# Moving V's store and class loads to the end of a batch, and a second buffer for the rows that are scattered to the experts

## The chip, the cores and the metric

The kernel runs on one core of one Trainium2 chip. The time is device time in microseconds (us) of one execution, and lower is better. A core has four compute engines, each with its own instruction queue that it works through in order: PE (TensorE, matrix products into PSUM), DVE (VectorE), ACT (ScalarE) and POOL (GpSimd). SP (SyncE) computes nothing here. It issues nearly all DMAs, and when it waits for a semaphore, every DMA behind that wait in its queue waits too. POOL issues the indirect DMAs, those whose destination rows are given by a list.

## The reference, cut to what matters

A block of attention with a gate, a layer norm, then a mixture of eight experts and a second layer norm. There are 16 batches of 512 tokens with 256 features and 16 heads of 16. Each token attends to 39 fixed distances back: 0 to 32 ("near") and 48, 64, 96, 128, 192, 256 and 384 ("far").

```python
scores = jnp.stack([jnp.einsum('bhnd,bhnd->bhn', q, _shift(k, delta, n)) for delta in OFFSETS], axis=-1) * scale
scores = scores + pos_bias.T[None, :, None, :]
alpha = jax.nn.softmax(scores, axis=-1)
for i, delta in enumerate(OFFSETS):
    out = out + alpha[..., i:i + 1] * _shift(v, delta, n)
gate = jax.nn.sigmoid(x @ Wgate + bgate)
return flat * gate @ Wout + bout
...
logits = jax.nn.relu(x @ rw1 + rb1) @ rw2 + rb2
vals, ids = jax.lax.top_k(logits, K)                 # K = 2
disp = jnp.zeros((E, CAP, Cx), x.dtype).at[ids_f, pos_c].add(xr * keep[:, None])
h = jax.nn.relu(jnp.einsum('enc,ech->enh', disp, ew1) + eb1[:, None, :])
eo = jnp.einsum('enh,ehc->enc', h, ew2) + eb2[:, None, :]
y = eo[ids_f, pos_c] * (probs_f * keep)[:, None]
...
x = _layernorm(x + _L0_attn_ref(x, L0_attn_Wqkv, ...), axis=-1)
x = _layernorm(x + _L0_ffn_ref(x, L0_ffn_rw1, ...), axis=-1)
```

## The kernel before

**Stages.** `attention` handles the 16 batches one after another, as a software pipeline, and leaves each token's normed row in DRAM twice: in `xln` (float32), and as a row of `disp`, at the place of its expert. `experts` then multiplies the rows of `disp` expert by expert, `combine` adds and norms. The change touches only `attention`, which is some three quarters of the time.

**The order of the work.** An iteration of the pipeline has 16 slots. `SLOTS_OF` says which steps stand in which slot, `AHEAD` to which batch a step belongs: in iteration i the projections are those of batch i+1 (`proj`), the max pass that of batch i+1 (`maxp`), scores and values those of batch i, the output product and layer norm those of batch i-1 (`outp`), the router that of batch i-1 (`rout`), ranks and scatters those of batch i-2 (`rank`). `run_iterations` writes each engine's instructions in that order. PE takes a step in its own slot, the other engines one slot later (or as `LATER` says). The engines keep pace by semaphores alone. Batch numbers of even and odd kind use two sets of buffers where a tile is a list (`n.par`).

**The steps that matter here, in the order of one iteration.**
- The max pass (`maxp` near0 to near3, far0, far1). For each block PE opens two PSUM banks with a bias matmul (L679) and adds many small products of q and k (L689). DVE reduces both banks (L954, L958). There are three banks (`gp`) for all such work, taken in turn. So near2 takes the last free bank and the one that DVE gives back when it has reduced the first half of near1.
- The far values. PE multiplies the far weights with `v_far` (L623) in slots 2 and 4. ACT copies them out of PSUM to `o_far`. They lie in another order of rows than the near ones, so SP stores them to `o_dram` (L442, four DMAs) and loads them back in the right order to `o_back` (L445). DVE's merge (L898) adds them to the near values into `ob`; the first merge of a batch waits for `o_back`.
- V. The projection leaves V in the tile `vs`. SP loads it to `v_near` (L434, 16 DMAs, at slot 1), stores it to `v_dram` (L459), waits until that has landed, and loads `v_far` from it in rows by class (L466, four DMAs). Before, these last two steps stand in SP's queue right behind the loads of q and k (`qs`, `ks`, L486) and ahead of `o_dram`.
- The mask rows. The maxima go through `m_dram` to one row of `qs` (L492, L496) at slot 12.
- The layer norm's end. ACT writes the normed rows to `y32` (L854, four instructions), then their float16 high part to `y16` (L859), and DVE the low part (L979). L859 may overwrite `y16` only when the scatters of the batch before have read it, and so waits for them.
- The scatters. POOL issues eight indirect DMAs a batch from `y16` to `disp` (L1095), behind the four small instructions of the layer norm of the next batch, and right before ACT's L859 of that batch is due.
- The gate. DVE computes the divisor and its reciprocal in the tile `oden` (L932, L937, each in two halves), and `og = ob * 1/oden` (L922).

These are the two waits of L859 and DVE's instruction behind it:

```python
wait(act, scattered, n.at(128))
...
act.wait_ge(y_ready, n.at(4, 4))
nc.scalar.copy(y16[:, :, 0:D], y32[:, :, :]).then_inc(yh_ready, 1)
...
dve.wait_ge(yh_ready, n.at(1, 1))
nc.vector.tensor_tensor(y16[:, :, D:2 * D], y32[:, :, :], y16[:, :, 0:D], ALU.subtract).then_inc(yl_ready, 1)
```

## Time and profile before

| | us |
|---|---|
| median of three runs | 2224.62 |
| the three runs | 2222.07 to 2226.25 |
| the profiled execution | 2221.11 |
| its span in the profile | 2219.4 |
| PE busy | 1547.7 (70%) |
| DVE busy | 968.8 (44%) |
| ACT busy | 907.2 (41%) |
| POOL busy | 662.7 (30%) |
| mean granted PE clock, share of 2.4 GHz | 0.774 |

The profile lists every instruction with its start and length. Where an engine stood idle, it also names what ended the wait, as in `[4.61 <-DVE m_near L954]`: 4.61 us idle until DVE's instruction of line 954 was done. "issue" as a cause means that the profile shows nothing that the engine waited for. In SP's rows the length is that of issuing the DMA, not of moving the data. L numbers are lines of the kernel before; after the change they are smaller by one from L310 on, and by other amounts further down (L859 is then L858, L679 is L678).

### The profile page before, as it was taken

Reading aid. Unit: us, or ns where it says so; the run is one execution under the profiler, and the core shown is the slowest. Engines: PE = TensorE matmul, PEld = TensorE weight load, DVE = VectorE, ACT = ScalarE, POOL = GpSimd, SP = SyncE. Lnnn points to the kernel's source line nnn. Section 1 sums busy time; section 2 is a strip of 40 time slices with the busy share of each in tenths; the row PEclk is TensorE's granted clock in tenths of the full one; section 3 lists DMA queues with packets and bytes.
Section 4 is the critical chain, followed back from the end, with each engine's and each line's share of the span. In section 5 each row is a group of like instructions: output and inputs, shape, how many; then the busy total and the mean of one; then the engine's idle time right before and its main releaser. Section 6 shows DMA issues by size and latency. Waiting matters only on the chain. (4 is left out here: it accounts for less than half of the span.)

```text
span 2219.4 us, 76239 instructions
## 1 busy us (share of the span) xinstructions
PE 1547.7 (70%) x33280; PEld 1043.3 (47%) x33280; DVE 968.8 (44%) x1925; ACT 907.2 (41%) x1544; POOL 662.7 (30%) x654
## 2 busy tenths in 40 slices
PE   0456686867768686867679686867864499999900
PEld 0234454545445454545445454545542267676700
DVE  4214354444534453544545354544533355555422
ACT  1132262534434262534435252534432365656323
POOL 4121232324141333324142333324132122323232
PEclk9676686868777796868778686868776699999955
DMA  2473433525151533425151523416010434444255
GB/s 79 95 207 98 99 77 84 97 71 122 47 123 37 114 66 85 88 70 104 49 125 42 101 66 78 96 47 128 22 44 12 126 75 108 86 104 89 28 136 184
DMA packets 238550, 194.80 MB, mean 88 GB/s; under 512 B 66847, under 2 KB 231727, under 8 KB 238080
## 3 DMA queue, kind: packets, MB, share of 16 engines
q1 hardware_dynamic: 222896, 175.11, 32.8%
q0 software_dynamic: 15360, 15.10, 4.2%
q8 instruction: 266, 4.36, 0.8%
q14 instruction: 28, 0.23, 0.0%
HBM read 98.07 MB, written 86.18 MB: 83 GB/s over the span
## 5 line engine op out<-in xcount | busy, mean ns | idle before, releaser
L395 POOL TENSOR_TENSOR p<-p 128x512 f16<-128x512 f32 x96 | 135.0, 1406 | 604.1 <-ACT p L791 563.0
L805 ACT COPY featT<-gp 128x1024 f16<-128x1024 f16 x96 | 93.4, 1032 | 354.2 <-PE gp L540 354.2
L395 DVE TENSOR_TENSOR p<-p 128x512 f16<-128x512 f32 x96 | 95.0, 990 | 286.5 <-ACT p L791 286.2
L547 PE MATMUL gp<-featT,wr 128*128 128x512 f16 x768 | 192.9, 409 | 24.1 <-DVE mT L947 18.2
L623 PE MATMUL o<-v_near,p 128*32 128x34 f16 (+1 forms) x6144 | 161.6, 185 | 36.3 <-issue 33.6
L623 PEld LDWEIGHTS o<-v_near,p 128*32 128x32 f16 x6144 | 153.7, 98 | 54.4 <-issue 51.2
L1387 PE MATMUL up<-rowsT,w 128*128 128x512 f16 x768 | 172.9, 386 | 8.8 <-DVE w L1464 5.3
L1401 PE MATMUL dn<-w,h 128*128 128x256 f16 x1536 | 170.1, 273 | 0.0
L1349 POOL DMA_INDIRECT xln<-y,place x64 | 104.9, 1640 | 217.5 <-DVE y L1491 176.7
L790 ACT ACTIVATE p<-st 128x512 f16<-128x512 f32 x192 | 116.6, 607 | 107.6 <-PE st L591 103.4
L1401 PEld LDWEIGHTS dn<-w,h 128*128 128x128 f16 x1536 | 149.7, 98 | 17.3
L1095 POOL DMA_INDIRECT disp<-y,sidx x128 | 126.7, 990 | 76.7 <-issue 49.4
L898 DVE TENSOR_TENSOR ob<-o,o_back 128x272 f32<-128x272 f32 x64 | 28.1, 439 | 260.9 <-DMA o_back<-o_dram 159.8
L1448 ACT ACTIVATE h<-up,b 128x512 f16<-128x512 f32 x128 | 88.1, 689 | 129.9 <-PE up L1387 73.1
L547 PEld LDWEIGHTS gp<-featT,wr 128*128 128x128 f16 x768 | 76.0, 104 | 123.8 <-issue 33.4
L1387 PEld LDWEIGHTS up<-rowsT,w 128*128 128x128 f16 x768 | 75.9, 99 | 99.9 <-issue 11.3
L591 PE MATMUL st<-qs,ks 49*64 49x32 f16 (+1 forms) x4096 | 104.3, 195 | 23.2 <-issue 23.2
L1503 DVE TENSOR_TENSOR h<-h 128x512 f16<-128x512 f32 x128 | 88.7, 693 | 69.6 <-ACT h L1449 69.6
L1082 POOL TENSOR_TENSOR x<-xin,x 128x1024 f16<-128x1024 f32 x16 | 34.0, 2128 | 281.2 <-ACT x L812 281.2
L791 ACT ACTIVATE p<-st 128x512 f32<-128x512 f32 x192 | 118.0, 615 | 0.0
L679 PE MATMUL gp<-near_bias,sel 32*128 32x512 f16 x96 | 28.9, 561 | 125.8 <-DVE m_near L954 124.3
L547 PE MATMUL gp<-wout,featT 128*128 128x256 f16 x384 | 79.2, 400 | 50.7 <-ACT featT L805 50.7
(173 smaller groups left out, 3067.1 us busy)
## 6 DMA issues: line engine op xcount, KB each, us to landing
qk_dram<-qk SPq DMA_DIRECT2D x64, 256.0 KB, 2.5
v_near<-vs SPq DMA_DIRECT2D x224, 66.0 KB
qs<-qk_dram SPq DMA_DIRECT2D x96, 128.0 KB, 4.6
ks<-qk_dram SPq DMA_DIRECT2D x96, 128.0 KB, 7.6
o_dram<-o_far SPq DMA_DIRECT2D x64, 136.0 KB
o_back<-o_dram SPq DMA_DIRECT2D x16, 544.0 KB
v_dram<-vs SPq DMA_DIRECT2D x16, 528.0 KB, 9.5
v_far<-v_dram SPq DMA_DIRECT2D x64, 132.0 KB
```

What stands on the lines that cost most here:

```text
L395: engine.tensor_tensor(p16[:, b, 1, :], p32[:, b, :], p16[:, b, 0, :], ALU.subtract).then_inc(is_split, 1)
L547: last = nc.tensor.matmul(dst, lhs(a, c), rhs(b, c), start=(k == 0), stop=(k == len(todo) - 1))
L591: last = nc.tensor.matmul(banks[e][64 * u + first:64 * (u + 1), P * z + BLOCK * b:P * z + BLOCK * (b + 1)], key[rows[e], p, lo - BLOCK + f ...
L623: last = nc.tensor.matmul(dst[quad, :, 2 * z + e, 0:cols.stop - cols.start], p16[:, 2 * (k % 2) + e, a, c:c + BLOCK], v[:, :, 2 * z + e, c ...
L790: nc.scalar.activation(p16[:, b, 0, :], bank[:, :], ACT.Exp)
L791: nc.scalar.activation(p32[:, b, :], bank[:, :], ACT.Exp).then_inc(exp_ready, 1)
L805: gp_done(nc.scalar.copy(featT[:, i, :, :].rearrange("f c t -> f (c t)"), bank[:, :].bitcast(F16)), n, stage, PART_OF_T[stage], i)
L1095: nc.gpsimd.indirect_dma_start(out=disp[:, :], out_offset=bass.IndirectOffsetOnAxis(ap=sidx[:, t, k:k + 1], axis=0), in_=y16[:, t, :].bitc ...
L1349: nc.gpsimd.indirect_dma_start(out=xln[:, :], out_offset=bass.IndirectOffsetOnAxis(ap=place[:, gr, t:t + 1], axis=0), in_=y[:, gr, t, :], ...
L1387: last = nc.tensor.matmul(up[h % 4][:, :], w1[e.par][:, a, c, P * h:P * (h + 1)], rowsT[:, gr, b, c, :], start=(k == 0), stop=(k == 5))
L1401: last = nc.tensor.matmul(dn[u][:, D * (t % 2):D * (t % 2 + 1)], h16[:, gr, a, h, P * t:P * (t + 1)], w2[e.par][:, b, h, :], start=(k == 0 ...
L1503: nc.vector.tensor_tensor(h16[:, gr, 1, h, :], h32[:, h % 2, :], h16[:, gr, 0, h, :], ALU.subtract).then_inc(h_lo, 1)
```

## The change

There are three parts.

1. V's store and class loads (`v_dram`, `v_far`) leave the step `proj vg1` and become `move_v`, called at the end of SP's step `maxp t`, behind the mask rows. They serve the same batch as before, and in the same iteration, eight slots later.
2. `y16` becomes a list of two tiles, taken in turn by the batch's number. ACT's L859 now waits for the scatters of the batch before the last (`n.at(128, -128)` in place of `n.at(128)`).
3. The tile `oden` goes. The gate's divisor and reciprocal are computed in `og` itself; in return the first divisor, no longer the product, waits for `og_lo` (that POOL has read the old `og`). It gives back the room that the second `y16` takes.

```diff
-        y16 = sb("y16", [P, TILES, ROW], F16)
+        y16 = [sb(f"y16_{i}", [P, TILES, ROW], F16) for i in range(2)]
-        oden = sb("oden", [P, TILES * H, HD], FP32)
...
             def proj(n, part):
-                if part == "vg0":
+                if part[:2] != "qk":
                     return
-                if part == "vg1":
-                    wait(sp, v_far_in, n.at(64, -64))
-                    sp.wait_ge(v_split, n.at(TILES, TILES))
-                    sync.dma_start(v_dram[n.par]...).then_inc(v_stored, 16)
-                    sp.wait_ge(v_stored, n.at(16, 16))
-                    wait(sp, pv_done, n.at(UNIT_PAIRS, FAR_PAIRS - UNIT_PAIRS))
-                    for u in range(2):
-                        for v in range(2):
...
             def maxp(n, part):
...
+                move_v(n)
+
+            def move_v(n):
+                wait(sp, v_far_in, n.at(64, -64))
+                sp.wait_ge(v_split, n.at(TILES, TILES))
+                sync.dma_start(v_dram[n.par]...).then_inc(v_stored, 16)
+                sp.wait_ge(v_stored, n.at(16, 16))
+                wait(sp, pv_done, n.at(UNIT_PAIRS, FAR_PAIRS - UNIT_PAIRS))
+                for u in range(2):
+                    for v in range(2):
...
-                    wait(act, scattered, n.at(128))
+                    wait(act, scattered, n.at(128, -128))
-                    nc.scalar.copy(y16[:, :, 0:D], y32[:, :, :]).then_inc(yh_ready, 1)
+                    nc.scalar.copy(y16[n.par][:, :, 0:D], y32[:, :, :]).then_inc(yh_ready, 1)
...
                 if part == "mul":
-                    wait(dve, og_lo, n.at(1))
...
                     if first == 0:
                         dve.wait_ge(eg_ready, n.at(TILES, TILES))
-                        wait(dve, og_ready, n.at(1))
+                        wait(dve, og_lo, n.at(1))
```

The other uses of `y16` (PE's transposes, DVE's low part and the tail with token and weights, POOL's scatters) take `y16[n.par]`; the clearing of `disp` takes `y16[0]`.

SP's queue, inside the loop, from the loads of q and k of the next batch to the mask rows. Before, V's two steps stand ahead of `o_dram`:

```order
L486 DMA qs<-qk_dram 16x8x512 x6
L486 DMA ks<-qk_dram 16x8x512 x6
L459 DMA v_dram<-vs 128x4x528
...
L466 DMA v_far<-v_dram 32x16x132 x4
...
L442 DMA o_dram<-o_far 128x1x272 x4
...
L445 DMA o_back<-o_dram 128x4x272
...
L501 DMA xln<-y 128x4x256
...
L450 DMA xres<-in_L_attn_x 128x4x256
...
L492 DMA m_dram<-mT 16x512
L496 DMA qs<-m_dram 1x4096 x2
```

After, at the same place of SP's queue:

```order
L471 DMA qs<-qk_dram 16x8x512 x6
L471 DMA ks<-qk_dram 16x8x512 x6
...
L441 DMA o_dram<-o_far 128x1x272 x4
...
L444 DMA o_back<-o_dram 128x4x272
...
L500 DMA xln<-y 128x4x256
...
L449 DMA xres<-in_L_attn_x 128x4x256
...
L477 DMA m_dram<-mT 16x512
...
L481 DMA qs<-m_dram 1x4096 x2
L488 DMA v_dram<-vs 128x4x528
...
L495 DMA v_far<-v_dram 32x16x132 x4
```

V's two steps moved past the way of the far values, the rows of the layer norm, the residual's load and the mask rows, and now stand ahead of the load of x and of `v_near` of the next iteration.

ACT, in an iteration written out ahead of the loop (an even batch), from the copy of the transposed rows to the next exponentials. Before:

```order
L805 COPY featT<-gp1 128x1024
L854 ACTIVATE y32<-y32,nmr,rstd 128x256 x4
L859 CAST y16<-y32 128x4x256
L790 ACTIVATE p16<-st0 128x512
L791 ACTIVATE p32<-st0 128x512
```

After:

```order
L804 COPY featT<-gp1 128x1024
L853 ACTIVATE y32<-y32,nmr,rstd 128x256 x4
L858 CAST y16_0<-y32 128x4x256
L789 ACTIVATE p16<-st0 128x512
L790 ACTIVATE p32<-st0 128x512
```

Nothing moved there; only the buffer of the copy is one of two, and an odd batch takes `y16_1`.

## Rows read from the trace of the kernel before

**Rows 1.** Waits of PE, 232:1630 us: total us, times, longest:
```profile
PE gp L679 <- DVE m_near L954: 105.5, 28, 13.5
PE gp L689 <- issue: 54.9, 83, 2.0
```

**Rows 2.** Waits of ACT, 232:1630:
```profile
ACT y L859 <- DMA disp<-y,sidx: 152.6, 13, 14.2
```

**Rows 3.** Timeline of PE, one batch: start, us, instruction, [idle before <- who ended it]:
```profile
856.34 0.76 PE L689 MATMUL gp<-ks,qs 16*32 16x64 f16 x58 [1.17 <-issue]
861.71 0.61 PE L679 MATMUL gp<-near_bias,sel 32*128 32x512 f16 x2 [4.61 <-DVE m_near L954]
...
864.39 0.61 PE L679 MATMUL gp<-near_bias,sel 32*128 32x512 f16 x2 [1.40 <-DVE m_near L954]
```

**Rows 4.** Timeline of DVE, the same batch:
```profile
855.22 0.44 DVE L898 TENSOR_TENSOR ob<-o,o_back 128x272 f32<-128x272 f32 x1 [12.38 <-DMA o_back<-o_dram]
859.83 1.23 DVE L979 TENSOR_TENSOR y<-y 128x1024 f16<-128x1024 f32 x1 [4.17 <-ACT y L859]
860.97 1.28 DVE L954 TENSOR_REDUCE m_near<-gp 128x8 f16<-128x512 f32 x2
```

**Rows 5.** Timeline of ACT, the same batch:
```profile
844.02 2.07 ACT L854 ACTIVATE y<-y,nmr,rstd 128x256 f32<-128x256 f32 x4 [10.15 <-POOL nmr L1078]
858.75 1.04 ACT L859 CAST y<-y 128x1024 f16<-128x1024 f32 x1 [12.66 <-DMA disp<-y,sidx]
```

**Rows 6.** Timeline of POOL, first and last of eight scatters:
```profile
844.83 1.11 POOL L1095 DMA_INDIRECT disp<-y,sidx  x1 [0.84 <-issue]
...
853.89 0.97 POOL L1095 DMA_INDIRECT disp<-y,sidx  x1 [0.30 <-issue]
```

**Rows 7.** Timeline of SP's queue, the same batch:
```profile
831.99 0.38 SPq L459 DMA_DIRECT2D v_dram<-vs  x1
...
844.44 2.77 SPq L442 DMA_DIRECT2D o_dram<-o_far  x4
850.71 0.39 SPq L445 DMA_DIRECT2D o_back<-o_dram  x1
...
890.25 0.54 SPq L496 DMA_DIRECT2D qs<-m_dram  x2
...
903.17 12.51 SPq L434 DMA_DIRECT2D v_near<-vs  x16
920.21 5.65 SPq L474 DMA_DIRECT2D qk_dram<-qk  x4
```

**Rows 8.** The line that stores v_dram (L459):
```profile
DMA to landing us min/median/max: 8.7/9.5/12.7
```

**Rows 9.** Timeline of PE, the first two batches:
```profile
170.72 0.61 PE L679 MATMUL gp<-near_bias,sel 32*128 32x512 f16 x2 [15.20 <-DVE m_near L954]
...
257.76 0.61 PE L679 MATMUL gp<-near_bias,sel 32*128 32x512 f16 x2 [7.97 <-DVE m_near L954]
...
259.92 0.61 PE L679 MATMUL gp<-near_bias,sel 32*128 32x512 f16 x2 [0.88 <-DVE m_near L954]
```

**Rows 10.** Timeline of PE, product for q and k:
```profile
908.71 0.29 PE L564 MATMUL st<-sel,far_bias 64*128 64x256 f16 x2 [2.85 <-ACT p L791]
...
912.13 7.71 PE L547 MATMUL gp<-featT,wqk 128*128 128x512 f16 x24
```

**Rows 11.** Timeline of POOL, near the end:
```profile
1641.10 1.15 POOL L395 TENSOR_TENSOR p<-p 128x512 f16<-128x512 f32 x1 [4.28 <-ACT p L791]
```

**Rows 12.** Timeline of ACT, the last batch:
```profile
1708.27 1.04 ACT L859 CAST y<-y 128x1024 f16<-128x1024 f32 x1 [12.52 <-DMA disp<-y,sidx]
```

**Rows 13.** Timeline of SP's queue, the next two o_back:
```profile
954.80 0.39 SPq L445 DMA_DIRECT2D o_back<-o_dram  x1
...
1051.83 0.39 SPq L445 DMA_DIRECT2D o_back<-o_dram  x1
```

**Rows 14.** Windows of 5 us (busy us of each engine, granted PE clock, DMA):
```profile
910.00:915.00 5.00, 3.81 (x71) 1.74 (x72) 3.15 (x1) 0.00 (x0) 0.79 (x1) 0.51 0.36 82
```

More of the change, by code:

```diff
@@ L496, in maxp @@
                     sync.dma_start(qs[n.par][r:r + 1, :, :], m_dram[n.par][PAIRS * e:PAIRS * (e + 1), :].unsqueeze(0)).then_inc(m_in[n.par], 16)
+                move_v(n)
+            def move_v(n):
+                wait(sp, v_far_in, n.at(64, -64))
+                sp.wait_ge(v_split, n.at(TILES, TILES))
+                sync.dma_start(v_dram[n.par].rearrange("(t p) c -> p t c", p=P), vs[n.par][:, :, :, :].rearrange("p t h c -> p t (h c)")).then_inc(v_stored, 16)
+                sp.wait_ge(v_stored, n.at(16, 16))
+                wait(sp, pv_done, n.at(UNIT_PAIRS, FAR_PAIRS - UNIT_PAIRS))
+                for u in range(2):
+                    for v in range(2):
+                        r, h = 64 * u + BLOCK * v, 8 * u + 4 * v
+                        src = v_dram[n.par][:, h * VW:(h + 4) * VW].rearrange("(a r) c -> a r c", r=FAR_STEP)
+                        sync.dma_start(v_far[r:r + BLOCK, :, u, v, :, :].rearrange("a r h c -> a r (h c)"), src).then_inc(v_far_in, 16)
             def outp(n, part):
@@ L928, in gate @@
                         dve.wait_ge(eg_ready, n.at(TILES, TILES))
-                        wait(dve, og_ready, n.at(1))
+                        wait(dve, og_lo, n.at(1))
                     dve.wait_ge(merged, n.at(TILES, end))
                     weight = ob[:, :, :, HD:OW].rearrange("q t h c -> q (t h) c")[:, heads, :]
-                    nc.vector.scalar_tensor_tensor(oden[:, heads, :], eg[n.par][:, heads, :], 1.0, weight.to_broadcast([P, H * (end - first), HD]),
+                    nc.vector.scalar_tensor_tensor(og[:, heads, :], eg[n.par][:, heads, :], 1.0, weight.to_broadcast([P, H * (end - first), HD]),
                                                    ALU.add, ALU.mult).then_inc(og_step, 1)
@@ L1118, in sem @@
             return ctx.enter_context(nc.semaphore(name))
-        ident, zero_rows = g["ident"], a["y16"]
+        ident, zero_rows = g["ident"], a["y16"][0]
         near_vec, far_vec = g["near_vec"], g["far_vec"]
```

25 lines of the change are left out of this document (10 added, 15 removed).

## The prediction

> **What bounds the kernel now.** Start with the page. No engine is near full: PE is busy for 70% of the span, DVE and ACT for less. So waits set the time of the attention stage, and they have to be read batch by batch. A batch takes about 100 us there, and the stage lasts roughly from 60 to 1720 us. The chain of waits on the page is no help: it ends in the last stage and reaches back only to 2129 us. I therefore went to the waits of PE, the engine that does most and whose order is fixed. In the 14 batches from 232 to 1630 us PE's largest wait is that of L679, the bias matmul that opens a block of the max pass, for DVE's reduction L954: 105.5 us in 28 waits. The second is not for anything the profile names: 54.9 us of "issue" before the small matmuls of L689 [rows 1]. ACT's wait at L859 for the rows that are scattered is 152.6 us in 13 batches, 11.7 us each [rows 2].
>
> Now follow one batch back from L679. PE finishes the block near1 at 857.1 us (856.34 + 0.76) and starts near2 only at 861.71, after 4.61 us [rows 3]. It waits for DVE's reduction of near1, which begins at 860.97. In front of that reduction, in DVE's order, stand two other instructions: L898, which waited 12.38 us for o_back, and L979, which waited 4.17 us for ACT's L859 [rows 4]. L859 stood 12.66 us until the scatters of the batch before had landed [rows 5]; POOL had begun to issue them at 844.83 and ended at 854.86 [rows 6]. So two waits lie one behind the other in front of DVE's reduction: o_back until 855.22, then the scatters until 858.75. The later one decides, and that is the scatters. From L859 to near2 it is always the same 3.0 us (861.71 - 858.75).
>
> **The two buffers.** With them L859 waits for the scatters of two batches ago, which ended about 90 us earlier. It then follows the four L854 at 846.1 us (844.02 + 2.07) and ends at 847.1. That cover is long; this wait is gone in every batch from the third on.
>
> **V's moves.** They decide when o_back comes. Now SP issues v_dram at 831.99, holds until it has landed, issues the four v_far, only then the four o_dram (844.44) and at 850.71 o_back, which lands 4.5 us later [rows 7]. Without V's steps SP can issue o_dram right at 832, as o_far was copied by then. It queues behind the ks loads exactly as v_dram does now, which lands after 9.5 us [rows 8], at 841.5. I take the same for o_dram: o_back issued at about 842 and landed at about 846.5, that is 8.7 us earlier. DVE then does the merge at 846.9, L979 by 848.4, and is idle before near1 is finished.
>
> So near2 waits for near1 itself and the first half of its reduction. An idle DVE makes that wait 0.88 us (at 259.92) [rows 9].
>
> **Where V's steps go.** They now stand behind the mask rows (890.25) [rows 7]. Issued at about 891, with at most the longest landing of any v_dram, 12.7 us [rows 8], and 2.9 us for v_far (from 841.5 to 844.44 now), SP is free at 906.6, or at 903.4 with the median. What stands behind them in SP's queue: the load of x, needed most of a batch later, and v_near, which starts at 903.17 now since it waits for PE. v_near takes 12.5 us of issue and ends 4.5 us before qk_dram is issued (920.21). So up to 4.5 us of delay are covered, and the longest landing makes 3.4 plus 0.4 for the load of x. The class products that need v_far come after the product that ends at 919.8 [rows 10]; v_far is issued by 906.6 and has 13 us to land. I put the move at nothing in the new place.
>
> **The gate in place** has the same four instructions and the same sizes. The wait for og_lo moves one step forward to work that ended tens of us before. Nothing.
>
> **What a batch gains.** The 28 waits of [rows 1] are 14 pairs. One pair is that of 257.76 and 259.92 (7.97 and 0.88) [rows 9]; in the other 13 the second wait is 1.40 [rows 3], together 18.2. That leaves 78.5 us for 13 first waits, 6.0 each. If each becomes 0.88 and each second one too, a batch gains 5.2 + 0.5 = 5.7 us. This is the upper end. The lower end comes from the "issue" waits. In the batch shown they end about 2 us after the last scatter was issued (854.86, and near1 ends at 857.1), and all along the scatters PE gets only a few matmuls at a time. In batches where near1 comes through early, near2 would meet the same trouble, and part of the gain is paid back. The batch shown, where near1 ends after the scatters, is not open to that: it gains 4.61 - 0.88 = 3.7 us, with the second wait 4.2. I take 3.7 for the lower end and 4.7, the middle, for the forecast: 13 x 4.7 = 61 us (48 to 74).
>
> **The batches at either end.** In the first, L679 waits 15.20 us at 170.72 for a reduction behind o_back [rows 9]. V's move brings o_back forward by 8.7 us, as in any batch. I take 9 (5 to 12). In the second there are no scatters yet, and 7.97 becomes 0.88: 7 us. In the last batch that has scores, POOL waited 4.28 us for ACT's exponentials behind L859 [rows 11]; its scatters had ended by 1636.8: 4 us. In the last of all nothing else runs: L859 waited 12.52 us [rows 12], and the router, the last scatters and the start of the experts all follow it. 12.5 us in full.
>
> **Sum:** 61 + 9 + 7 + 4 + 12.5 = 93.5 us. The profiled execution took 2221.1 us (span 2219.4), the sum makes it 2127.6. The median of the runs is 2224.6, 3.5 above it, so my forecast is **2131 us**, 4.2% less.
>
> **Rivals.**
>
> *The clock takes it back, or doubles it.* Batches differ although their work is the same: from o_back to o_back one takes 104.1 us and the next 97.0 [rows 7, 13]. One reason in view is the product for q and k. In the long batch it ran from 912.13 for 7.71 us, while from 910 to 915 the granted clock was 0.51, the lower of the two levels (1.2 GHz); PE had waited 2.85 us for ACT just before [rows 10, 14]. The change shifts every phase, so all batches could be long ones (about 3.5 us more than the mean, 13 x 3.5 = 46: 2177) or short ones (2085). The waits in front of that product are not touched, which speaks for no change. 0.12 and 0.10.
>
> *POOL's scatters are slowed by DVE.* Now DVE is idle while POOL issues them, from 842.8 to 855.2. After the change the merge (0.44), L979 (1.23), the reduction (1.28) and a split fall into these 10 us. If each held POOL for its whole length, the last scatter would come 3 to 4 us later, and the "issue" waits with it: 13 x 3.5 = 45 us of the gain lost, 2176. No row shows a DVE instruction beside a scatter in this stage, so it can't be excluded, and the length that I give it, 3.5 us, is that of these instructions. 0.10.
>
> The Trainium skill has the rule that speaks for this case (SBUF — State Buffer, section "SBUF: two separate sides"): DVE and GpSimd share a pair of ports under an exclusive lock, and descriptors written by GpSimd starve while DVE holds it. The section names DVE operations with two SBUF inputs only against a GpSimd operation that reads SBUF; by that, of the four, only L979 and the split could count, and the time would be about 2156, an estimate from their lengths; no row here shows it.
>
> *The wait for o_back stays.* If o_dram lands late (it is four DMAs where v_dram is one), the merge could come at 852 instead of 847. DVE would still be done with L979 and ready at about 853.7, before near1 ends at 857.1. It costs only the batches where near1 comes early, about 2 us in five of them: 2141. Inside the range. So V's move by itself should be worth only the two first batches, some 16 us, and the buffers the rest; this is a point the experiments can test.
>
> *Slower than before.* V's steps in the new place hold SP, and v_near, the q/k store, the key loads and PE's near0 shift in turn. Each us beyond the cover of 4.5 costs one us a batch. To eat the 93.5 us it needs 7.2 us in each of 13 batches on top of the cover: SP free no earlier than 914.9, 24 us after v_dram was issued, where the longest landing and the issue in the trace make 15.6. At 10 us beyond the cover the time would be 2261. 0.04.
>
> **How the numbers follow.** Forecast with its own spread of 2110 to 2155: 0.62. Scatters slowed 0.10, all batches long 0.12, all short 0.10, slower 0.04, and 0.02 for no change by a cause I don't see. The range of eight in ten goes from 2092 to 2178. About 0.2% is what a measurement of this kernel can tell from no change. Faster by more: 0.93; within: 0.02; slower: 0.05.
>
> **What would show it.** In the profile of the changed kernel ACT's L858 must have no wait for the scatters; o_back must land about 2 us after the values of near0, not 11; the wait of L678 for the reduction must be near 0.9 us in place of 6.0, with "issue" waits as before; and the batch must take about 95 us. If "issue" waits in front of the small matmuls grow by as much as the waits for DVE shrink, the scatters are the bound and my lower end is too high. If the scatters take longer than 10.0 us for eight, DVE slows them. If PE waits more for ks, V's steps hold SP. It would be wrong altogether if PE had another chain of the same length behind DVE's reduction, which I do not find in its waits.

## The result, and the profile after

| | us |
|---|---|
| kernel before, median of the runs beside it | 2223.35 |
| kernel after, median of four runs | 2152.39 (2149.35 to 2154.96) |
| ratio after to before, 95% interval | 0.9681 [0.9661, 0.9702] |
| span of the profiled execution, before and after | 2219.4 and 2152.9 |

The change saves 71 us, 3.2%. The forecast was 2131, so the sign is right and the time is within the range, but it is 21 us above the forecast: of the 93.5 us expected 22 did not come (27 by the two spans).

First the waits of PE from 232 to 1630 us in the kernel after, the same view as [rows 1] (total us, times, longest). L678 is the bias matmul, L688 the small matmuls, L952 DVE's reduction:

```profile
PE gp L678 <- DVE m_near L952: 66.2, 28, 7.2
PE gp L688 <- issue: 54.1, 93, 1.2
```

The wait for DVE fell from 105.5 to 66.2 us, the "issue" waits stayed where they were (54.9). The wait of ACT for the scatters [rows 2] is gone from the list. Two rows are new. "remote" is what the view says when a semaphore's increment ended the wait, but the instruction that makes this increment had ended long before:

```profile
DVE m_near L952 <- remote: 60.2, 9, 8.5
ACT p L789 <- remote: 11.1, 9, 2.2
```

Now one batch of the kernel after, at the place of [rows 3 to 6]. ACT (L853 is the normed rows, L858 the float16 copy):

```profile
817.33 2.07 ACT L853 ACTIVATE y<-y,nmr,rstd 128x256 f32<-128x256 f32 x4 [10.09 <-POOL nmr L1076]
819.43 1.04 ACT L858 CAST y<-y 128x1024 f16<-128x1024 f32 x1
```

POOL, the first, third and last of the eight scatters:

```profile
818.14 1.10 POOL L1093 DMA_INDIRECT disp<-y,sidx  x1 [0.85 <-issue]
...
820.83 1.75 POOL L1093 DMA_INDIRECT disp<-y,sidx  x1 [0.30 <-issue]
...
827.99 0.97 POOL L1093 DMA_INDIRECT disp<-y,sidx  x1 [0.30 <-issue]
```

DVE (L897 merge, L977 low part, L952 reduction of near1):

```profile
819.61 0.44 DVE L897 TENSOR_TENSOR ob<-o,o_back 128x272 f32<-128x272 f32 x1 [3.45 <-DMA o_back<-o_dram]
820.51 1.23 DVE L977 TENSOR_TENSOR y<-y,y 128x1024 f16<-128x1024 f32 x1 [0.46 <-issue]
830.35 1.29 DVE L952 TENSOR_REDUCE m_near<-gp 128x8 f16<-128x512 f32 x2 [8.61 <-PE gp L688]
```

PE, the end of near1, and near2:

```profile
821.72 0.44 PE L688 MATMUL gp<-ks,qs 16*32 16x64 f16 x26 [0.24 <-issue]
...
828.59 0.27 PE L688 MATMUL gp<-ks,qs 16*32 16x64 f16 x5 [1.16 <-issue]
830.04 0.24 PE L688 MATMUL gp<-ks,qs 16*32 16x64 f16 x2 [1.19 <-issue]
831.10 0.61 PE L678 MATMUL gp<-near_bias,sel 32*128 32x512 f16 x2 [0.81 <-DVE m_near L952]
```

Both waits of the old chain are gone: L858 follows L853 without a wait, the merge comes 1.5 us after the first scatter instead of 10.4 (855.22 - 844.83), and DVE is done by 821.7. Then it waits 8.61 us for PE. PE issues its matmuls two to eight at a time with gaps of 0.45 to 1.19 us, until 1.1 us after the last scatter was issued (828.96). near2 opens 13.0 us after the first scatter.

The batch before it shows the other face of the same thing. There near1 comes through (PE), and DVE begins late:

```profile
728.35 0.27 PE L688 MATMUL gp<-ks,qs 16*32 16x64 f16 x4 [0.48 <-issue]
734.99 0.60 PE L678 MATMUL gp<-near_bias,sel 32*128 32x512 f16 x2 [6.37 <-DVE m_near L952]
```

```profile
724.68 1.23 DVE L977 TENSOR_TENSOR y<-y,y 128x1024 f16<-128x1024 f32 x1 [3.58 <-issue]
734.24 1.29 DVE L952 TENSOR_REDUCE m_near<-gp 128x8 f16<-128x512 f32 x2 [8.34 <-remote]
```

The eight scatters of this batch stand from 722.32 to 733.13. near1 is finished at 728.6 (the view models the ends of matmuls) and DVE is idle, yet its reduction begins at 734.24, 1.1 us after the last scatter again. DVE could not begin earlier: the trace records the semaphore increment that it waits for at 734.22, 5.6 us after the end of the matmul that makes it. Outside the scatters such an increment stands at most 0.09 us after its matmul's end in this trace; in the nine batches with a "remote" wait of DVE it comes 2.2 to 6.4 us late. I call this time, from some 1.5 us after the first scatter until 1.1 us after the last, **the window**. In 10 of 13 batches near2 opens 12.7 to 13.1 us after the first scatter. In the other three it slips in before, and then near3 waits until 13.0 to 13.4 us. Before the change near2 opened 16.0 us after it on the mean.

Where the 66.5 us of the two spans lie, by the start of scatters in POOL's timeline:

| stretch | before | after | saved | forecast |
|---|---|---|---|---|
| start to the first scatter (343.32, 336.12) | 343.3 | 336.1 | 7.2 | 16 |
| 12 batches, to 1543.90 and 1496.72 | 1200.6 | 1160.6 | 40.0 | 56 |
| the 13th and the last with scores (to 1694.27, 1640.24) | 150.4 | 143.5 | 6.9 | 8.7 |
| the last of all (to its last scatter) | 48.9 | 37.7 | 11.3 | 12.5 |
| the later stages | 476.2 | 475.0 | 1.2 | 0 |

### The profile page after: what moved, and what is told of

The parts are those of the page before. It is cut to its first block and busy times, and to the rows that moved or that the text cites. A ratio compares the mean times of both kernels' runs of the same rounds, so it can differ in the third digit from the quotient of the medians.

```text
span 2152.9 us, 76230 instructions
## 1 busy us (share of the span) xinstructions
PE 1557.9 (72%) x33280; PEld 1048.6 (49%) x33280; DVE 961.3 (45%) x1925; ACT 907.2 (42%) x1544; POOL 673.1 (31%) x654
## 3 DMA queue, kind: packets, MB, share of 16 engines
q8 instruction: 266, 4.36, 0.9%
## 5 line engine op out<-in xcount | busy, mean ns | idle before, releaser
L804 ACT COPY featT<-gp 128x1024 f16<-128x1024 f16 x96 | 93.5, 1034 | 439.0 <-PE gp L539 439.0
L394 DVE TENSOR_TENSOR p<-p 128x512 f16<-128x512 f32 x96 | 85.4, 890 | 297.3 <-ACT p L790 297.1
L546 PE MATMUL gp<-featT,wr 128*128 128x512 f16 x768 | 195.5, 413 | 24.5 <-DVE mT L945 18.2
L789 ACT ACTIVATE p<-st 128x512 f16<-128x512 f32 x192 | 116.8, 608 | 120.8 <-PE st L590 105.5
L1093 POOL DMA_INDIRECT disp<-y,sidx x128 | 137.6, 1075 | 65.3 <-issue 48.9
L952 DVE TENSOR_REDUCE m_near<-gp 128x8 f16<-128x512 f32 x128 | 81.9, 682 | 156.6 <-PE gp L688 96.3
L874 ACT ACTIVATE hid<-gp,br 128x512 f16<-128x512 f32 x128 | 88.8, 694 | 63.5 <-PE gp L546 60.4
L546 PE MATMUL gp<-featT,wqk 128*128 128x512 f16 x384 | 111.9, 461 | 1.4 <-ACT featT L804 1.2
```

The costliest lines, as they stand in the source:

```text
L394: engine.tensor_tensor(p16[:, b, 1, :], p32[:, b, :], p16[:, b, 0, :], ALU.subtract).then_inc(is_split, 1)
L546: last = nc.tensor.matmul(dst, lhs(a, c), rhs(b, c), start=(k == 0), stop=(k == len(todo) - 1))
L789: nc.scalar.activation(p16[:, b, 0, :], bank[:, :], ACT.Exp)
L804: gp_done(nc.scalar.copy(featT[:, i, :, :].rearrange("f c t -> f (c t)"), bank[:, :].bitcast(F16)), n, stage, PART_OF_T[stage], i)
L874: nc.scalar.activation(hid16[:, 0, ht, :], bank[:, :], ACT.Relu, bias=br1[:, ht:ht + 1], scale=1.0 / WS)
L1093: nc.gpsimd.indirect_dma_start(out=disp[:, :], out_offset=bass.IndirectOffsetOnAxis(ap=sidx[:, t, k:k + 1], axis=0), in_=y16[n.par][:, t, ...
```

## Experiments: the two halves of the change

**Buffers alone.** V's two steps put back where they stood:

```diff
                 if part == "vg1":
+                    wait(sp, v_far_in, n.at(64, -64))
+                    sync.dma_start(v_dram[n.par]...).then_inc(v_stored, 16)
...
-                move_v(n)
```

> The changed kernel with V's two steps put back ahead of o_dram; two y16 buffers and the gate in place stay. Theory A (the step of the prediction): the wait of ACT for the scatters was the later of two, so the buffers alone carry all batches with scatters, and V's move is worth the first two batches, about 16 us: 2168 us, 2160 to 2176. In the trace DVE's merge waits for o_back until 8 to 10 us after the first scatter, as before, and near2 opens 12.7 to 13 us after it, as in the changed kernel. Theory B: o_back decides as soon as the scatter wait is gone, then near2 opens later than 13 us and the time is above 2185 us.

Measured: 2151.43 us against 2228.18, ratio 0.965 [0.9628, 0.9671]. The time is that of the whole change, and 9 us below the range of the expectation, which had given about 16 us to V. From first scatter to first scatter a batch takes 95.3 us here and 96.7 in the kernel after: 17 us less in the 12 batches, against 12 us more at the start (first scatter at 348.2 here, at 336.1 after). One batch, DVE and PE (L895 merge, L950 reduction, L676 bias, L686 small matmuls):

```profile
833.60 0.44 DVE L895 TENSOR_TENSOR ob<-o,o_back 128x272 f32<-128x272 f32 x1 [12.50 <-DMA o_back<-o_dram]
```

```profile
826.15 0.60 PE L686 MATMUL gp<-ks,qs 16*32 16x64 f16 x11 [0.32 <-issue]
836.07 0.60 PE L676 MATMUL gp<-near_bias,sel 32*128 32x512 f16 x2 [9.32 <-DVE m_near L950]
```

PE finishes near1 at 826.75 and then waits 9.32 us for DVE, whose merge waits for o_back. In the kernel after o_back comes in time, and PE loses the same time to the window. In this batch one wait stands where the other stood. In seven of the 13 batches near2 opens earlier here, 8.9 to 10.9 us after the first scatter, and in the other six at 13.0 to 15.4.

The window itself is not in this trace, though the same rows are scattered at the same place. Among scatters that stand from 632.23 to 642.27, near1 comes in one piece:

```profile
635.18 0.78 PE L686 MATMUL gp<-ks,qs 16*32 16x64 f16 x64
```

The "issue" waits in front of the small matmuls are 8.9 us here, from 232 to 1630, and 54.1 in the kernel after; there is no "remote" wait of DVE. The next section comes back to this.

**V's move alone.** One `y16`, with the old wait:

```diff
-            y16 = [sb(f"y16_{i}", [P, TILES, ROW], F16) for i in range(2)]
+            y16 = [sb("y16", [P, TILES, ROW], F16)] * 2
-                    wait(act, scattered, n.at(128, -128))
+                    wait(act, scattered, n.at(128))
```

> The changed kernel with one y16 buffer and the old wait for the scatters of the batch before; V's move and the gate in place stay. Theory A: only the first two batches gain, about 16 us: 2207 us, 2200 to 2214, and L859's wait (here L858) stays near 11 us a batch, near2 opens about 16 us after the first scatter. Theory B (o_back decides): most of the 71 us are here, below 2180 us.

Measured: 2214.39 us against 2228.18, ratio 0.9951 [0.9927, 0.9975]: 14 us saved by the medians and 11 by the ratio, where the prediction had 16. ACT:

```profile
849.06 1.04 ACT L858 CAST y<-y 128x1024 f16<-128x1024 f32 x1 [10.66 <-DMA disp<-y,sidx]
```

PE:

```profile
838.12 0.61 PE L678 MATMUL gp<-near_bias,sel 32*128 32x512 f16 x2
852.02 0.61 PE L678 MATMUL gp<-near_bias,sel 32*128 32x512 f16 x2 [12.49 <-DVE m_near L952]
```

Again 3.0 us from L858 to near2, as in the kernel before. This confirms the chain of the prediction: with one buffer the scatters decide, however early o_back is. near2 opens 14.9 us after the first scatter (837.14). The parts do not add: 78 for the buffers and 11 for V by these ratios, 71 for both. (The kernel after was measured in another group of runs than these two; more on that below.)

**The gate in place alone.** The kernel before with `oden` gone and nothing else.

> The kernel before with the gate computed in place alone (one buffer, V's steps in their old place). Every theory: no change, 2222 to 2228 us, ratio 1.000 within 0.002, since the four instructions keep their sizes and the wait for og_lo falls on work that ended tens of us before. A difference of over 0.3% would mean that the in-place operands cost DVE or that the wait is not free.

Measured: 2227.24 us against 2226.28, ratio 1.000 [0.9978, 1.0023]. It costs nothing, as put down. But its trace has no window either: the "issue" waits in front of the small matmuls are 5.0 us from 232 to 1630, where the kernel before has 54.9. At one buffer this makes no difference to the time, as PE then waits for the scatters through L859 in any case.

## Experiments: what the window is

**No scatters.** The loop's scatters are left out but for those of the last batch; the waits for them go too. So the experts read rows that were not written.

```diff
+                    if not (n.i is None and n.c == B - 1):
+                        return
-                    wait(act, scattered, n.at(128, -128))
-                    wait(dve, scattered, n.at(128))
```

> The changed kernel, without the eight scatters of every batch but the last (the waits for them go too), and with one more wait between the two groups of adds in the expert stage; so only the attention stage up to the last batch is to be read. Theory C: while POOL's eight scatters run, PE and DVE get their next instructions late, and this window of 10.8 us is the floor that kept near2 at 12.7 us after the first scatter. Then without scatters near2 opens within 4 us of the place where the first scatter stood, the issue waits in front of the small matmuls of L688 fall from 54 us in 14 batches below 15, DVE's waits labelled remote vanish, and a batch takes 87 to 90 us in place of 96.7. Theory D: the late instructions come from the other DMAs around it (o_back, xln, xres) and not from the scatters: the issue waits stay above 40 us and a batch takes 95 us or more.

Measured in one run: 2052.28 us. From o_back to o_back a batch takes 89 us, there is no "remote" wait, and the longest wait for L952 is 3.3 us. So the kernel without scatters takes 100 us less than the kernel after, 7 us or so a batch, though no engine waits for one there. The experts' later stages are no part of this: from the last scatter to the end it is 474 to 478 us in this run, in the three below and in the kernel after.

**Small rows.** The same 128 indirect DMAs, with 64 bytes of each row to a table of its own in place of the 1040 to `disp`. What the experts read is again left out.

```diff
-                            out=disp[:, :], ...
-                            in_=y16[n.par][:, t, :].bitcast(U32), ...
+                            out=g["thin"][:, :], ...
+                            in_=y16[n.par][:, t, 0:32].bitcast(U32), ...
```

> The changed kernel with the same eight scatters a batch, the same number of rows and indices, but 64 bytes of each row in place of 1040, written to a table of their own; the rows of the experts stay empty, and the expert stage has one more wait between its adds, so only the attention stage is to be read. If the bytes in the DMA queues delay the instructions (theory C1), it looks like the kernel without scatters: batch 87 to 91 us, issue waits of L688 below 20 us. If the making of the descriptors on POOL or their number does it (theory C2), it looks like the changed kernel: batch 95 to 98 us, issue waits of L688 near 54 us, near2 at 12 us or later after the first scatter.

Measured in one run: 2060.80 us. POOL does the same work (eight scatters in 10.8 to 11.4 us, the third again 1.8 us), but near2 opens 4.3 us after the first. PE in the middle of the eight (782.41 to 793.75):

```profile
786.69 0.61 PE L679 MATMUL gp<-near_bias,sel 32*128 32x512 f16 x2 [2.37 <-DVE m_near L953]
787.22 0.74 PE L689 MATMUL gp<-ks,qs 16*32 16x64 f16 x64
788.85 0.61 PE L679 MATMUL gp<-near_bias,sel 32*128 32x512 f16 x2 [0.88 <-DVE m_near L953]
```

All 64 matmuls in one piece. So POOL's work, the number of its rows, and a lock between POOL and DVE do not make a window by themselves: all three are here, and it is not.

**Half rows and quarter rows.** The same, with 512 and with 256 bytes.

> As the kernel with 64 B of each row scattered to a table of its own, now with 512 B of each row (the experts again read rows that the loop did not scatter, and the output is not the reference's). 1040 B to disp gave 2152 us, 64 B gave 2061. Theory C1 in its proportional form (what starves PE is the volume of the scattered rows): half the volume, half the loss, about 2105 us, with starts of DVE delayed less often. Theory C1 with a threshold (the 16 DMA engines must be full for the starving; at half the bytes their queues drain between two scatters): 2060 to 2075 us and no DVE start late by over 2 us. Theory of the destination (writes into disp are what costs, not their size; both this and the 64 B one write elsewhere): 2061 us as well, so a time near 2105 rules both others out, a time near 2061 leaves two.

Measured in one run: 2145.46 us. All three forms of the expectation missed: with half the bytes nearly the whole loss is back (93 of 100 us). These rows too go to a table of their own, so writing to `disp` is not what it takes. PE, among scatters that stand from 720.79 to 731.92:

```profile
728.31 0.27 PE L689 MATMUL gp<-ks,qs 16*32 16x64 f16 x5 [0.48 <-issue]
729.04 0.27 PE L689 MATMUL gp<-ks,qs 16*32 16x64 f16 x6 [0.46 <-issue]
729.77 0.27 PE L689 MATMUL gp<-ks,qs 16*32 16x64 f16 x5 [0.46 <-issue]
...
733.70 0.61 PE L679 MATMUL gp<-near_bias,sel 32*128 32x512 f16 x2 [2.95 <-DVE m_near L953]
```

> As before with 64 and 512 B of each row, now 256 B (the experts again read rows that the loop did not scatter). 64 B: 2061 us, 512 B: 2145, 1040 B: 2152. The volume alone is out after those, since half of it takes nearly the whole loss. If the loss follows the size of one row with a step somewhere under 512 B: either 2060 to 2065 us (step above 256 B) or 2140 to 2150 us (step below). If it rises with the size and saturates, between: 2090 to 2125 us, with near2 opening 6 to 9 us after the first scatter where 64 B gave 4.3 and 512 B 12.8 in every second batch.

Measured in one run: 2070.74 us, near2 4.1 to 4.7 us after the first scatter in all 13 batches. So the four times fall in two pairs: 2061 and 2071 us with 64 and 256 bytes in a row, 2145 and 2152 with 512 and 1040.

**It is not the volume.** A row whose place lies beyond its expert's 1024 is dropped by the bounds check, and the trace's DMA packets carry 4 bytes for it in place of 1040. Later batches drop more and more rows: the packets of a batch's scatters hold 1.07 MB in the second batch of the kernel after, 0.62 in the sixth, 0.15 in the twelfth and 0.08 in the thirteenth. The window does not get shorter: near2 opens 13.0, 13.0 and 12.8 us after the first scatter in the first three of these, near3 13.4 us after it in the last. Three stretches of 11 us with the scatters (busy us and count of PE, PEld, DVE, ACT and POOL, granted PE clock, DMA share, GB/s). The second and the twelfth batch of the kernel after:

```profile
430.00:441.00 11.00, 4.05 (x90) 2.20 (x87) 1.58 (x2) 3.63 (x7) 8.85 (x9) 0.63 0.60 195
1402.00:1413.00 11.00, 3.57 (x96) 1.86 (x88) 1.67 (x2) 4.18 (x8) 8.87 (x9) 0.50 0.35 110
```

The second batch with 64 bytes in a row:

```profile
424.00:435.00 11.00, 6.88 (x366) 4.44 (x360) 6.11 (x9) 4.20 (x8) 8.85 (x9) 0.66 0.36 108
```

DMA share and GB/s are the same in the last two, while PE gets 96 matmuls in the one and 366 in the other.

The Trainium skill (DMA: Bandwidth & Descriptors, section "Specifications") says that a transfer under 512 B does not reach the line rate. That is about the transfer, and no run here measured the rate of these rows. The Trainium skill (SBUF — State Buffer, section "SBUF: two separate sides") also says that a DMA cannot be slowed by a compute operation, nor the other way round. In the window the single matmul keeps its length of some 0.2 us, but its start is late; whether the DMAs' traffic is what delays it, these runs do not show.

**A rival that these runs do not exclude.** The size of a row is not enough to make a window. The runs were taken in six groups, and the kernel before was timed beside each; groups 2 and 5 ran on the same chip, 75 minutes apart. By the "issue" waits in front of the small matmuls (232:1630) the window comes and goes with the group:

| group | kernels, with the issue waits in us | window |
|---|---|---|
| 1 | before 54.9, after 54.1 | yes |
| 2 | buffers only 8.9, V's move only 3.0, no scatters 3.0, 64 bytes 2.9 | no |
| 3 | gate only 5.0, slot 11 2.0, slot 11 with V back 4.8, spread 2.4 | no |
| 4 | spread with V back 7.6, first V 2.9 | no |
| 5 | 512 bytes 60.6 | yes |
| 6 | 256 bytes 1.7 | no |

Buffers only, V's move only and gate only scatter the full rows of 1040 bytes at the old place, and have no window. So two readings are left. Either the window needs rows of 512 bytes or more and something else that comes and goes with the kernel as it is built; or it comes and goes with the chip and the hour, and the pair of 2061 and 2071 against 2145 and 2152 says nothing of the size of a row. The kernel after was measured in group 1 alone, so nothing here decides between the two; it would take the kernel after and the one with 64 bytes side by side, several times. The time of the kernel before is no help: it is 2223 to 2229 us in every group, and that of gate only, without a window, is the same.

**What holds PE is open, but two candidates are weaker than they look.** The table of DMA queues has one of kind "instruction" (266 packets, 4.36 MB), so the engines' own instructions travel by DMA as well, and a refill behind the rows is a candidate. In the batch of the kernel after shown above a packet of that queue ran from 820.70 to 822.38 and the next began at 832.88; none was under way while PE was held, from 822.66 to 830.28, in which time it took 37 matmuls. In 12 of the 13 batches none is under way from 4.4 to 14.0 us after the first scatter. The other candidate is a late semaphore. It holds DVE, as said above; but of these 37 matmuls only one waits for a semaphore, and it is not in the first groups, which are as late. The last packet of the rows ends at 830.02, PE's first matmul after its last gap starts at 830.04.

## Experiments: the scatters elsewhere

With two buffers the scatters no longer have to be done before L858 of the next batch, so they can leave the max pass. `SLOTS_OF` is all that changes. The kernels of this section have no window, see the table above, and are compared below with a kernel after that has one.

**All in slot 11**, behind the max pass, and the same **with V's steps put back**:

```diff
-    6: [("outp", "w"), ("maxp", "near0"), ("rank", "s0"), ("rank", "s1")],
-    7: [("rank", "s2"), ("rank", "s3"), ("outp", "y"), ("maxp", "near1")],
+    6: [("outp", "w"), ("maxp", "near0")],
+    7: [("outp", "y"), ("maxp", "near1")],
-    11: [("maxp", "t"), ("rout", "h0")],
+    11: [("maxp", "t"), ("rout", "h0"), ("rank", "s0"), ("rank", "s1"), ("rank", "s2"), ("rank", "s3")],
```

> All eight scatters of a batch stand in slot 11 (behind the max pass) in place of slots 6 and 7; all else as in the kernel after. Theory P (place: their traffic costs because it falls on the max pass, where PE and DVE hand three banks to and fro; in slot 11 ACT's exponentials set the pace and there is slack): the window costs 2 us a batch or less in the new place, spacing of the batches about 90 to 92 us, 2152 - 13 x 5.5 = 2080 us, no waits of DVE's reduction for 'remote'. Theory A (amount: a window of 10 us costs PE the same 6 to 7 us wherever it lies): 2145 to 2155 us, with 'issue' waits on other lines of PE. A third outcome, slower than 2160, is POOL: it would be late with the splits of slot 12 and the values would wait for it (L622 for POOL).

> Scatters in slot 11 as in the other, and V's store and class loads put back ahead of o_dram. The merge then waits for o_back as it did, and with it DVE's reduction. If the new place of V's steps matters only once the scatters are out of the max pass: 13 x (near2 held until 3.7 us after the merge, some 2 to 4 us more than near1 needs) = 25 to 50 us more than with V's steps at the end, about 2105 to 2130 where that one gives 2080. If it is worth nothing in any company (as it was with the scatters in their old place): the same time as all in slot 11 within 0.3%, but for the first batch's 9 us.

Measured: 2091.50 us for the first, ratio 0.9386 [0.9356, 0.9417]; 2177.79 for the second, ratio 0.9784 [0.9749, 0.9818]. The first comes out 11 us above what the first theory (the place decides) gave. Its reason, slack in slot 11, is not what the trace shows: there is no window there at all, and no increment of PE's semaphores comes more than 0.1 us late beside the scatters. So the place, or what made the other kernels of groups 2 to 4 free of it, took the window away. The 11 us are in one row that the kernel after does not have (336:1497): POOL, busy with eight scatters in a row, is late with its share of the exponentials, and PE's values wait for it.

```profile
PE o L631 <- POOL p L403: 32.9, 12, 3.4
```

V's steps, which made no difference with the scatters in their old place, are worth 86 us here, far more than the 25 to 50 of the expectation. With V's steps back, slot 11 is 26 us slower than the old place (2178 against 2151).

**Spread over slots 11 to 14**, two DMAs in each, and the same **with V's steps put back**:

```diff
+    11: [("maxp", "t"), ("rout", "h0"), ("rank", "s0")],
+    12: [("rout", "h1"), ("gate0", "den0"), ("gate0", "inv0"), ("rank", "s1")],
+    13: [("rout", "h2"), ("rank", "s2")],
+    14: [("rout", "h3"), ("rank", "s3")],
```

> The four pairs of scatters of a batch stand in slots 11, 12, 13 and 14, two DMAs each, with POOL's own work between. Theory P as for all in slot 11, and the bytes spread over about 25 us in place of 10: 2070 to 2085 us, at or a little under the one with all in slot 11, and POOL is never late by more than 2 us. Theory A: 2145 to 2155 us. If the starving depends on the rate of bytes and not on their sum, this one is faster than all in slot 11 by over 5 us; if on the sum alone, they are equal.

> Scatters in slots 11 to 14 and V's steps back ahead of o_dram: the fourth corner of a square (scatters early or spread late, V's steps old or new place). The three others are 2151 (early, old), 2152 (early, new) and 2068 us (late, new). Theory A (V's move has a value of its own only if nothing else holds the max pass): as with all scatters in slot 11, where putting V's steps back cost 86 us, this one comes to 2068 + 86 = 2154 us, with the merge's wait for o_back at some 10 us a batch and PE's wait for DVE's reduction at 9. Theory B (the late place alone brings the gain, and the loss in the slot 11 pair was POOL's lateness meeting V's old place): 2075 to 2100 us.

Measured: 2067.78 us, ratio 0.9276 [0.9241, 0.9311], and 2138.90, ratio 0.9597 [0.9575, 0.962]. The second lies between its two theories (2154, and 2075 to 2100), nearer to the first. Spread, the wait for POOL is gone, and the kernel comes within 16 us of the one without scatters. The square, in us:

| | V's steps ahead of o_dram | V's steps at the end |
|---|---|---|
| scatters in slots 6 and 7 | 2151 | 2152 |
| scatters spread over 11 to 14 | 2139 | 2068 |

Neither move is worth more than 13 us by itself, together they are worth 84. PE's wait for DVE's reduction says what V's steps do (336:1497). Spread, V's steps at the end:

```profile
PE gp L687 <- DVE m_near L961: 49.1, 26, 3.6
```

Spread, V's steps back, PE and then DVE:

```profile
PE gp L685 <- DVE m_near L959: 117.2, 26, 9.6
```

```profile
DVE ob L904 <- DMA o_back<-o_dram: 133.4, 13, 12.7
```

With V's steps back the merge waits for o_back, and near2 for the merge. In the kernel after o_back comes in time, but the window holds near2 about as long. The two end within a few us of each other, so taking one away does not show while the other is there. It was so before the change, with L859's wait as a third.

Which of the square's two causes the late place removed is not settled. Only the corner of 2152 has a window. If the late place took it away, the place is worth 84 us. If it came with group 1, V's steps at the end are worth 71 to 91 us wherever the scatters stand (the kernel with 64 bytes in a row has the old place, V's steps at the end and no window, and takes 2061), and the place is worth little: 12.5 us with V's steps back.

**V's steps of the first batch alone in their old place**, on top of the spread kernel:

```diff
                 if part[:2] != "qk":
+                    if part == "vg1" and n.i is None and n.c == 0:
+                        move_v(n)
                     return
```

> The kernel with the scatters spread over slots 11 to 14, and V's two steps of the very first batch alone in their old place (ahead of the loop), all others at the end. Theory A (the term 'first batch' of the prediction failed because V's steps, put behind the first mask rows at 106 us, hold SP for 7 us there, where no cover exists, so that v_near, the q/k store and the ks loads come later): v_near issues at 107 in place of 114, the wait for ks at about 145 us shrinks from 14.0 to 9.7, near2 of the second max pass (168.1 in the kernel after) opens at 163.5 to 164.5 and the span is 4 to 5 us shorter, 2063 us. Theory B (the first batch's gain was taken by something else, and the wait for ks has another cause): no change of the time, ks wait as it was.

Measured: 2059.23 us, ratio 0.9235 [0.9215, 0.9256]. That is the fastest kernel of the study, 4.6% below the kernel after by the ratios. Its profiled span is 5.5 us shorter than the spread one's (2062.6 and 2068.1), as expected; the intervals of the two ratios overlap, so the gain itself rests on the rows below. SP's timeline shows the cause. Kernel after:

```profile
103.96 0.32 SPq L477 DMA_DIRECT2D m_dram<-mT  x1
...
105.97 0.39 SPq L488 DMA_DIRECT2D v_dram<-vs  x1
109.13 3.63 SPq L495 DMA_DIRECT2D v_far<-v_dram  x4
...
114.02 14.09 SPq L433 DMA_DIRECT2D v_near<-vs  x16
```

This kernel, with V's steps of the first batch at 74 us:

```profile
102.63 0.32 SPq L488 DMA_DIRECT2D m_dram<-mT  x1
...
105.69 13.58 SPq L442 DMA_DIRECT2D v_near<-vs  x16
```

From the mask rows to v_near it is 10.1 us in the one and 3.1 in the other. PE's wait for ks behind it, in the kernel before, in the kernel after and in this one:

```profile
144.61 0.61 PE L679 MATMUL gp<-near_bias,sel_rest 32*128 32x512 f16 x2 [9.71 <-DMA ks<-qk_dram]
```

```profile
149.26 0.61 PE L678 MATMUL gp<-near_bias,sel_rest 32*128 32x512 f16 x2 [13.99 <-DMA ks<-qk_dram]
...
168.14 0.61 PE L678 MATMUL gp<-near_bias,sel 32*128 32x512 f16 x2 [5.29 <-DVE m_near L952]
```

```profile
146.29 0.61 PE L690 MATMUL gp<-near_bias,sel_rest 32*128 32x512 f16 x2 [10.58 <-DMA ks<-qk_dram]
...
164.76 0.61 PE L690 MATMUL gp<-near_bias,sel 32*128 32x512 f16 x2 [5.38 <-DVE m_near L964]
```

## Why the prediction was right in sign and 21 us short

**The chain was right.** Both waits in front of DVE's reduction were found in the right order. V's move alone left near2 3.0 us behind L858, and two buffers took that wait away in every batch.

**The term that was mis-sized is the 13 steady batches, 61 us.** The lower end, 3.7 us, was worked out from a batch in which near1 ends after the scatters, and it holds: near2 there was to open 13.2 us after the first scatter (861.71 - 3.7 - 844.83), and it opens at 13.0. The upper end assumed that in batches where near1 comes early near2 opens early too. It does not: near2 or near3 waits for 13 us in every batch. near3 opened 18.6 us after the first scatter on the mean of the 13 batches and opens at 14.6 now, 4.0 us earlier; a batch gained 3.3 (40.0 / 12), a little less than the lower end. Taking the middle, 4.7, was the choice that failed. The prediction saw the sign of it (PE gets "only a few matmuls at a time" all along the scatters), and priced it as a doubt and not as a bound. It also looked at PE alone: in the kernel after the late increments hold DVE's reduction as well (60.2 us of "remote"). The waits of the kernel before have no such row, as DVE waited for o_back there, but its semaphores do: near1 ends at 755, and its increment comes 5.6 us later.

The sign that the prediction had set for this case did not show. It said that "issue" waits in front of the small matmuls would grow if the scatters were the bound. They stayed (54.9 and 54.1), since the window is in both traces; in the kernel without scatters they are 3.0.

That the time came within 1% of the forecast is in part luck. Both ends of 3.7 and 5.7 were read from a trace with a window in it. In the kernel with 64 bytes in a row, which has both changes and no window, the batches come every 89 us, where the kernel after takes 96.7.

**First and second batch: 16 expected, 7.2 measured at the first scatter.** In the first the wait for the reduction fell by 9.9 us (15.20 to 5.29), as put down, but near2 opens only 2.6 us earlier (170.72 to 168.14). Ahead of it PE's wait for ks grew from 9.71 to 13.99 us, and near0 opens 4.7 us later. The prediction worked out the cover for V's steps, 4.5 us of slack in SP's queue, from a batch of the loop, and did not look at the first one, which has none; with V's first steps in their old place near2 opens at 164.76, 3.4 us earlier. In the second the wait of 7.97 us became 0.90, as put down:

```profile
246.27 0.61 PE L678 MATMUL gp<-near_bias,sel 32*128 32x512 f16 x2 [0.90 <-DVE m_near L952]
```

near2 opens 11.5 us earlier there (257.76 to 246.27). Of these, 4.3 us are lost again before the first scatter. Two products behind it ran longer than before: one for the router 4.45 us in place of 2.76, that for q and k 7.95 in place of 6.84, 2.8 us together. The granted clock was 0.57 from 272 to 276 us, around the first, and 1.00 from 283 to 286 in the kernel before. The remaining 1.5 us I did not find.

**The end: 21.2 expected, 18.2 measured** (6.9 + 11.3), with the last batch's 12.5 good to 1.2 us.

**V's steps in the loop cost nothing**, as put down, and with more room than assumed: v_dram lands after 3.3 us in the new place, not 9.5 to 12.7 [rows 8], where only the mask rows stand ahead of it. PE's waits for ks from 232 to 1630 us stay at 4.7 us (4.9 before). SP's timeline and the landing of L488:

```profile
858.78 0.39 SPq L488 DMA_DIRECT2D v_dram<-vs  x1
862.43 2.60 SPq L495 DMA_DIRECT2D v_far<-v_dram  x4
...
869.35 13.19 SPq L433 DMA_DIRECT2D v_near<-vs  x16
887.02 5.66 SPq L459 DMA_DIRECT2D qk_dram<-qk  x4
```

```profile
DMA to landing us min/median/max: 3.0/3.3/3.5
```

**"V's move by itself is worth only the two first batches"** held beside one buffer (11 us), and was 0 beside two, in a comparison with a kernel after that has a window. It is no property of the move: beside the late scatters it is worth 71 to 86. The prediction summed the parts as if they were independent.

**The rivals.** *Scatters slowed by DVE*: true in kind, wrong in size. The eight take 10.8 us instead of 10.0, all of it in the one that stands beside L977 (1.75 instead of 0.97 us); the merge and the reduction did not show. By the Trainium skill (SBUF — State Buffer, section "SBUF: two separate sides") only the two operations with two SBUF inputs could count, and that is what the traces show: beside L977 here, and in the kernel with 64 bytes beside L978 (1.78 us) and a split (1.49 us). The estimate that went with it, 2156, is close to the time that came, but for another reason: 0.8 us a batch is the third scatter, and the missing gain is the window. *The clock*: the mean granted clock is 0.775 after 0.774, and batches still differ (93.1 to 99.0 us). It took a few us, not 46: the products for q and k and those of the router are busy for 307.4 us (111.9 and 195.5) in place of 301.5 (108.6 and 192.9), 2.8 of these 5.9 in the second batch. *The wait for o_back stays*: it does not, the first merge comes 1.9 us before to 2.1 us after the first scatter. *V's steps hold SP*: only in the first batch (4.7 us).

## What to carry to other kernels

When two or three waits end within a few us of each other, price a change by where the last of them moves to, and give no part a value of its own; a two-by-two of the parts shows it in four runs. Take the four side by side on one chip, the changed kernel among them, and look in each trace for the waits that the argument needs: here one corner has a window that the others lack, and the square cannot tell place from window. A buffer that removes a wait can be worth more for the freedom it gives than for the wait: with it the scatters could leave the stretch where PE and DVE pass banks to and fro, and that kernel is 84 us faster, for whichever of the two causes. A cover that is worked out for the loop has to be worked out again for the first iteration.

## What the hardware showed that was not expected

In three of the 14 traces (the kernels before and after, and the one with 512 bytes in a row) a window stands beside the eight indirect DMAs of a batch. In it PE is given only a few matmuls per 0.73 or 1.45 us, and the semaphore increments of PE's matmuls are recorded up to 6.4 us after their ends, until 1.1 us after the last scatter was issued. It is as long with 0.08 MB of rows moved as with 1.07 MB, and at a DMA share of 0.35, at which a kernel with 64 bytes in a row (0.36) has none. Five kernels with the full rows in the max pass were traced, and three of them (buffers only, V's move only, gate only) have no window either; what turns it on is open.

In the profile it reads as "issue" and "remote" waits: an engine that waits for nothing that can be seen, beside a row of indirect DMAs, is a reason to search every trace that one compares for the same waits.
